# Value product of the attention by whole heads: 512-column matmuls in four parts, landing buffers for two heads

## The reference

```python
C_q = Q @ Wq_d                                  # [4, 512, 128]
C_kv = K @ Wkv_d                                # [4, 1601, 64]
CqWqk = (C_q @ W_qk).reshape(b, n, 16, 64)
scores = jnp.einsum('bnhl,bkl->bhnk', CqWqk, C_kv) / 8
attn = jax.nn.softmax(scores, axis=-1)
V_up = (C_kv @ Wv_u).reshape(b, nkv, 16, 64)
out = jnp.einsum('bhnk,bkhd->bnhd', attn, V_up)
```

## Time and profile before

| what | us |
|---|---|
| timed runs, median (lowest, highest) | 2739.88 (2732.51, 2740.12) |
| the profiled execution's own time | 2740.16 |
| its span, first to last instruction | 2738.2 |
| mixer and start of the attention | 324.55 |
| the 255 steps of the attention, first to last second-half score product | 1078.08 |
| from there to the first matmul of the feed-forward network | 27.61 |
| feed-forward network | 1307.96 |

### The profile page before, as it was taken

One profiled execution on the slowest core, in us unless ns is written; L12 is line 12 of the kernel. 1 busy time (PEld: TensorE's weight loads), 2 busy tenths in 40 slices (PEclk: granted clock), 3 DMA queues, 4 the chain that ended last, 5 costly groups with the idle time before them and its releaser, 6 DMA issues.

```text
span 2738.2 us, 42011 instructions
## 1 busy us (share of the span) xinstructions
PE 2602.3 (95%) x14328; PEld 1979.5 (72%) x14328; DVE 2315.4 (85%) x2664; ACT 1670.2 (61%) x2619; POOL 1966.1 (72%) x1473
## 2 busy tenths in 40 slices
PE   7998899999999999999988999999999999999997
PEld 4665666666666666666656888888888888788885
DVE  2766688989998999899857999899998899899988
ACT  3444687877787778787855445454455555555553
POOL 1002377677777778777857999999887888888883
PEclk9899999999999999999999999999999999999999
DMA  7426677687778776877681222112223222132221
GB/s 276 157 100 206 212 236 216 188 240 206 223 214 261 206 219 204 259 228 221 201 278 69 100 93 93 70 70 70 77 70 123 77 85 78 70 116 79 83 93 77
DMA packets 166792, 420.64 MB, mean 154 GB/s; under 512 B 30130, under 2 KB 57652, under 8 KB 166068
## 3 DMA queue, kind: packets, MB, share of 16 engines
q1 hardware_dynamic: 164276, 409.57, 47.2%
q10 hardware_dynamic: 2304, 8.39, 0.8%
HBM read 248.43 MB, written 75.04 MB: 118 GB/s over the span
## 4 chain that ended last, share of the span: by engine, by line
PE 44%; SPq 3%; DVE 2%; POOL 1%; issue 1%; ACT 1%; DMA 1%; POOLq 0%; ACTq 0%; DVEq 0%
PE c_ps L1610 42%; SPq L912 2%; PE c_ps L1622 1%; DVE c_sum_g L1766 0%; DVE c_stats L1826 0%; DMA c_ident<-in_ident 0%; POOL b_rw L1357 0%; PE c_ps L1631 0%; POOL c_sum_g L1851 0%; PE b_po L1038 0%; PE b_sc L1019 0%; DVE c_acc L1766 0%; DMA b_rz<-in_c_dz 0%; DMA b_rz<-in_c_gz 0%; ACT c_sg L1674 0%
## 5 line engine op out<-in xcount | busy, mean ns | idle before, releaser
L1766 DVE SCALAR_TENSOR_TENSOR c_acc<-c_ps,c_sd,c_acc 128x1024 f32<-128x1024 f32 x440 | 562.9, 1282 | 90.8 <-PE c_ps L1610 90.7
L1668 ACT ACTIVATE c_scaled<-c_ps,c_sgu 128x1024 f32<-128x1024 f32 x336 | 375.2, 1117 | 422.5 <-PE c_ps L1610 414.7
L1101 ACT ACTIVATE b_pr<-b_sc,b_nm 128x799 f32<-128x799 f32 (+1 forms) x512 | 477.7, 935 | 169.4 <-DVE b_pr L1190 146.9
L1851 POOL TENSOR_TENSOR c_sum_u<-c_sum_u,c_scaled 128x1024 f32<-128x1024 f32 x168 | 404.8, 2410 | 99.6 <-ACT c_scaled L1668 98.3
L1851 POOL TENSOR_TENSOR c_sum_g<-c_sum_g,c_scaled 128x1024 f32<-128x1024 f32 x168 | 405.1, 2411 | 73.2 <-ACT c_scaled L1668 72.2
L1019 PE MATMUL b_sc<-b_kh,b_qs 128*128 128x402 f32 (+1 forms) x1024 | 398.6, 389 | 45.0 <-ACT b_pr L1101 41.2
L1197 DVE STREAM_TRANSPOSE b_tn<-b_pr 128x1280 f32<-128x1280 f32 x256 | 385.4, 1506 | 28.7 <-ACT b_pr L1101 14.6
L1315 POOL COPY b_pt<-b_tn 32x640 f32<-32x640 f32 x430 | 307.4, 715 | 141.7 <-DVE b_tn L1197 82.5
L1019 PE MATMUL b_sc<-b_kl,b_qs 128*128 128x402 f32 (+1 forms) x1024 | 355.9, 348 | 0.0
L1766 DVE SCALAR_TENSOR_TENSOR c_sum_g<-c_ps,c_sgu,c_sum_g 128x1024 f32<-128x1024 f32 x224 | 286.4, 1278 | 26.0 <-PE c_ps L1610 20.6
L1190 DVE TENSOR_SCALAR_CACHE_REDUCE b_pr<-b_sc,b_nm_first 128x799 f32<-128x799 f32 x256 | 268.7, 1050 | 29.1 <-PE b_sc L1019 8.3
(11 more groups left out here) (212 smaller groups left out, 4871.0 us busy)
## 6 DMA issues: line engine op xcount, KB each, us to landing
b_pt<-b_tn SPq DMA_DIRECT2D x774, 80.0 KB, 2.7
shared<-b_tn SPq DMA_DIRECT2D x378, 80.0 KB, 2.8
c_uw_int<-wint_u SPq DMA_DIRECT2D x56, 512.0 KB, 3.5
c_gw_int<-wint_g SPq DMA_DIRECT2D x56, 512.0 KB, 3.4
c_dw_int<-wint_d SPq DMA_DIRECT2D x56, 512.0 KB, 3.4
a_cx<-in_b_ctxT SPq DMA_DIRECT2D x16, 1608.0 KB, 9.8
b_rw<-in_c_gw SPq DMA_DIRECT2D x28, 512.0 KB, 4.1
b_rz<-in_c_gz SPq DMA_DIRECT2D x28, 512.0 KB, 5.6
```

The costliest lines, as they stand in the source:

```text
L1101: S.activation(pr[u % 2][:, k0:k1], sc[:, at + lo:at + hi], ACT.Exp, bias=nm[:, u % 2:u % 2 + 1], accum_out=den[:, g % 2, q, half:half + 1 ...
L1668: S.activation(dst[:, :], pair[SLOT[x, t] % 4][:, :], ACT.Identity, scale=scale(x, t)).then_inc(s_e, 1)
L1766: V.scalar_tensor_tensor(out=total, in0=pair[SLOT[x, t] % 4][:, :], scalar=scale(x, t), in1=before, op0=ALU.mult, op1=ALU.add).then_inc(s_ ...
L1851: G.tensor_tensor(total, total, scaled[m % 2][:, :], ALU.add).then_inc(s_add, 1)
```

## The change

The value product is made per head. `weigh(g, part)` takes the four units of a head together, 512 columns in each matmul, 13 matmuls per head, in four parts over four steps: tiles 10 to 12 (those that PE turned), then 0 to 3, 4 to 6 and 7 to 9. The half of `b_po` is chosen by a running count (`z = n % 2`). The first part stands in steps 7 and 3 (`WEIGH_AT = 7`), the last in steps 2 and 6. The copy of the product out of PSUM moves one step later (`LATENT_AT = 10`, steps 2 and 6); the output product stays in steps 3 and 7.

The landing buffers hold two heads (`b_pt` and a part of `shared`): a mover may start on a pair when the head two before has been weighed, and PE waits for the two pairs of a head at once, in its second part. `b_pe` has two buffers of a head, freed after the first part by a semaphore of its own. To make room, `b_ot` and some small tiles move into `shared`, tiles of the feed-forward network are laid out in another order, its first gate weights are loaded at the end of the attention's last pair and no longer in the pairs before, and some semaphores of the mixer are merged. The weight blocks skip pairs 17, 20, 23 and 26 of a batch and no longer 20 to 23.

```diff
-FREE = (2, 5, 8, 11, 14, 20, 21, 22, 23, 30, 31)
+FREE = (2, 5, 8, 11, 14, 17, 20, 23, 26, 30, 31)
-WEIGH_AT = 6
-LATENT_AT = 9
+WEIGH_AT = 7
+WEIGH_PARTS = [(10, 11, 12), (0, 1, 2, 3), (4, 5, 6), (7, 8, 9)]
+LATENT_AT = 10
 OUT_AT = 11
-MOVES = 3
...
+        def landing(p, a, c):
+            z = p % 2 * 2
+            return pt[p // 2 % 2][32 * c:32 * c + 32, a, z:z + 2, :]
+
+        def landing_free(eng, p):
+            if p >= 4:
+                eng.wait_ge(s_pv, p // 2 - 1)
...
-            def weigh(p, part):
-                b, s, g = p // 2 // HEADS, p % 2, p // 2
+            def weigh(g, part):
+                b = g // HEADS
                 if part == 0:
-                    moved(T, p)
-                    T.wait_ge(s_pe, 2 * p + 2)
-                    if s == 0 and g:
+                    T.wait_ge(s_pe, UNITS * (g + 1))
+                    if g:
                         T.wait_ge(s_ot, g)
...
-                for t in (range(0, 7), range(7, NKT))[part]:
-                    z = t % 2
+                elif part == 1:
+                    moved(T, 2 * g)
+                    moved(T, 2 * g + 1)
+                for n, t in enumerate(WEIGH_PARTS[part], sum(len(x) for x in WEIGH_PARTS[:part])):
+                    z = n % 2
...
-                    ins = T.matmul(po[z * LAT:(z + 1) * LAT, s * 256:(s + 1) * 256], cn[:, b, t, :], turned,
-                                   start=(t < 2), stop=(t >= NKT - 2))
-                if part == 1:
+                    ins = T.matmul(po[z * LAT:(z + 1) * LAT, :], cn[:, b, t, :], turned,
+                                   start=(n < 2), stop=(n >= NKT - 2))
+                if part == 0:
+                    ins.then_inc(s_pa, 1)
+                elif part == len(WEIGH_PARTS) - 1:
                     ins.then_inc(s_pv, 1)
...
             def out_latent(g):
-                S.wait_ge(s_pv, 2 * g + 2)
+                S.wait_ge(s_pv, g + 1)
...
-FIRST = [("u", 0), ("g", 0)]
+FIRST = [("u", 0)]
...
                     Q.dma_start(sgu[:, :, :], d["gus"]).then_inc(s_scales, 16)
+                    load("g", 0)
```

More of the change, by code:

```diff
@@ L221, in sync @@
                 Q.wait_ge(s_kvout[k], 4 * 4 * 16)
-            Q.wait_ge(s_early, 32)
+            Q.wait_ge(s_wts, 64)
         def tensor():
-            T.wait_ge(first, 32)
             for l in range(L):
-                T.wait_ge(xin[l + 1 if l else 0], 16)
+                T.wait_ge(xin[l + 1 if l else 0], 16 if l else 48)
                 for c in range(KC):
@@ L409, in scalar @@
                     S.wait_ge(small, 10 * 16)
[L410 to L413, removed]
+                    S.wait_ge(s_prep, 3)
+                    S.activation(alog[:, :], alog[:, :], ACT.Exp).then_inc(s_soft, 1)
+                    S.activation(g1[:, :], g1[:, :], ACT.Sigmoid).then_inc(s_soft, 1)
+            S.wait_ge(s_prep, 6)
             def keep_context(pair):
@@ L859, in attention @@
         tn = [sb(f"b_tn{j}", [P, 4, 2, SEG]) for j in range(2)]
-        pt = [sb(f"b_pt{j}", [P, 4, 2, SEG]) for j in range(2)]
-        pt.append(shared[:, NXC + 2 * NSZ - 8 * SEG:NXC + 2 * NSZ].rearrange("p (a z e) -> p a z e", a=4, z=2))
-        pe = [sb(f"b_pe{j}", [P, NKT - NDT, 2, P]) for j in range(3)]
-        ot = sb("b_ot", [P, NB])
+        pt = [sb("b_pt0", [P, 4, UNITS, SEG])]
+        end = NXC + 2 * NSZ
+        pt.append(shared[:, end - 16 * SEG:end].rearrange("p (a u e) -> p a u e", a=4, u=UNITS))
+        ot = shared[:, end - 16 * SEG - NB:end - 16 * SEG]
+        pe = [sb(f"b_pe{j}", [P, NKT - NDT, UNITS, P]) for j in range(2)]
         yo = sb("b_yo", [P, 2, QT, LAT])
@@ L866, in attention @@
         nm0 = sb("b_nm_first", [P, 2])
-        den = sb("b_den", [P, 2, QT, 2])
-        rd = sb("b_rd", [P, 2, QT])
+        small = shared[:, end - 16 * SEG - NB - 32:end - 16 * SEG - NB]
+        den = small[:, 0:16].rearrange("p (a q z) -> p a q z", a=2, q=QT)
+        rd = small[:, 16:24].rearrange("p (a q) -> p a q", a=2)
+        var, step = small[:, 24:28], small[:, 28:32]
         stats = sb("b_stats", [P, QT, 2, 6])
@@ L1104, in keep_turned @@
             def keep_turned(u):
+                g = u // UNITS
                 S.wait_ge(s_tr, u + 1)
-                if u >= 6 and u % 2 == 0:
-                    S.wait_ge(s_pv, u // 2 - 2)
-                S.copy(pe[u // 2 % 3][:, :, u % 2, :], mi[:, 0:(NKT - NDT) * P].rearrange("p (t e) -> p t e", e=P)).then_inc(s_pe, 1)
+                if g >= 2 and u % UNITS == 0:
+                    S.wait_ge(s_pa, g - 1)
+                S.copy(pe[g % 2][:, :, u % UNITS, :], mi[:, 0:(NKT - NDT) * P].rearrange("p (t e) -> p t e", e=P)).then_inc(s_pe, 1)
             def cross(p):
@@ L1465, in ffn @@
         sgu = sb("c_sgu", [P, 2 * KC, NI])
-        part = {n: [sb(f"c_sum_{n}{j}", [P, HALF]) for j in range(2)] for n in "gu"}
-        scaled = [sb(f"c_scaled{j}", [P, HALF]) for j in range(2)]
         sg = sb("c_sg", [P, HALF])
-        h = sb("c_h", [P, HALF])
         stats = sb("c_stats", [P, OR, 2, 6])
@@ L1472, in ffn @@
         rstd = sb("c_rstd", [P, OR])
-        d1 = sb("c_dw_int1", [P, HID], F32R)
-        w = {"g": [sb("c_gw_int0", [P, HID], F32R)], "u": [sb("c_uw_int0", [P, HID], F32R)]}
-        for n in "gu":
+        h = sb("c_h", [P, HALF])
+        w = {n: [sb(f"c_{n}w_int0", [P, HID], F32R)] for n in "ug"}
+        part = {n: [sb(f"c_sum_{n}{j}", [P, HALF]) for j in range(2)] for n in "gu"}
+        scaled = [sb(f"c_scaled{j}", [P, HALF]) for j in range(2)]
+        for n in "ug":
             w[n].append(sb(f"c_{n}w_int1", [P, HID], F32R))
-        w["d"] = [sb("c_dw_int0", [P, HID], F32R), d1]
+        w["d"] = [sb(f"c_dw_int{j}", [P, HID], F32R) for j in range(2)]
         xs = sb("c_xs", [P, XR, HID])
```

85 lines of the change are left out of this document (40 added, 45 removed).

## The result

The changed kernel takes 2751.4 us (median of 13 runs, 2743.7 to 2754.8) against 2739.9 (13 runs): a ratio of 1.0040, 95% interval 1.0028 to 1.0052, so 8 to 14 us slower. The prediction was 2754. The profiled execution of after took 2746.63 us, only 6.5 us more than the profiled one of before; its span, 2744.3, is 6.1 us longer. What is missing to the 11.5 us of the medians lies ahead of the attention, whose second-half score of step 0 starts at 318.44 in place of 324.55, 6.1 us earlier. What follows compares stages and steps, not spans.

A forecast was written before the change was run, and what follows sets the result against it. The attention was where time could move, with no engine near its limit. 0.66 us per cycle over 32 cycles gave 21 us, less 7 for landing buffers: +14 on 2740.2, so 2754 us, with 2741 to 2773 for 8 in 10.

The forecast's parts named there:

- Step 7: Attention's regular eight-step cycle: PE fills this step, so 0.42 us more, plus a new 0.12 us wait of `output` for ACT's copy.
- step 3: Attention's regular cycle: PE fills this step, so 0.42 us more, less 0.09 us for a restart that goes; no new wait.
- steps 1 and 2: Attention's regular cycle: PE's wait for ACT's exponential goes, so 7.86 us becomes 7.67, a gain of 0.19.
- steps 5 and 6: Attention's regular cycle: the chain from ACT's copies of the queries keeps its length, so 8.75 us stays; change 0.
- steps 0 and 4: Attention's regular cycle: value product of four matmuls takes 1.86 us instead of 1.87, so 0.01 us less each.
- Weight blocks: Attention's weight-block copies and their pair spacing: 0, at worst 2 us in each of three batches.
- Landing buffers: Attention's irregular part, 25 us outside the regular cycle: slack for every second pair and longer pairs take back 7 us.
- the irregular time: Rival: all 25 us outside the attention's regular cycle go, giving 2736 us; chance 0.13 (most of it, 2734 to 2748).
- The lone matmul found no partner: Rival, value product: next instruction's records run beside the odd matmul, giving 2720 us; chance 0.06, shared with other waits gone.
- The cheap wide record: Rival, value product: 512 columns take only 0.215 us, DVE then holds the attention, giving 2672 us; chance 0.01.
- no odd step hides anything: Rival, attention: odd steps pass on PE's added work and `output` waits 0.35 us, cycle 2.0 us longer, 2804 us; chance 0.07.
- The hidden ending: Attention's end: last head's landed tiles take 4.3 us instead of 3.0, hidden by the 3.9 us wait before the feed-forward network.

## Why the prediction was right, and where it wasn't

The value product came out term by term. Step 7 grew by 0.60 us (0.42 and the wait of 0.12 predicted, 0.18 measured), step 3 by 0.32 (0.33 predicted), steps 1 and 2 fell by 0.21 (0.19), steps 5 and 6 stayed at 8.74, steps 0 and 4 are unchanged: 0.71 us a cycle against 0.66, 22.7 us against 21. The reason is shown three ways: taking a lone matmul away (steps 3 and 7, 0.856 us), halving it by a split in both halves (0.42), and making one half deeper (0.85). PE's busy time grew by 42 us and not by the 52 of work: for one, step 1 of before counts as busy for the whole of its 3.55 us, of which the prediction found 3.42 to be work. Of the 42 us by which PE's busy time grew, 29 filled waits for ACT that are gone (41.2 to 12.4), and the other 13 lengthen the stage.

Two small terms were wrong, and that they cancelled is luck. "Weight blocks" stood at 0, and was worth 7 to 9 us to the good. "Landing buffers" stood at -7, a gain that no run shows: with the old spacing the irregular part didn't shrink (26.8 against 25.1), though the times leave room for it. The step that failed is the reading of the earlier trace rows: it was seen that row loads push the exchange back, not that a block in the same pair, whose store has to land, makes SyncE's turn longer than the pair (9.04 us against 8.44), nor that `FREE` decides how many such pairs follow each other. For the spacing only POOL's normalised rows were weighed.

Of the rivals, the irregular time did pay some, 9 of 25 us, by another mechanism than the one argued. The lone matmul found no partner by itself. Given one by a split in the same parts it brings less than that case priced: a cycle of 32.89, where it foresaw some 32.6, and 2733 us in place of 2720; 2716.5 took the parts 3, 3, 4, 3 as well. The cheap wide record is refuted. The Trainium skill's price for a matmul alone (TensorE: Matmul & The Clock Gate, section Back-to-back issue gap), which the prediction says the records follow, fits them in proportion to the columns only: as an estimate by it 512 columns would take 0.216 us, and a record takes 0.43. That no odd step hides anything is refuted too: the cycle grew by 0.71 and not by 2.0 us, since steps 1 and 2 need 7.65 us, less than the 7.86 of before. The hidden ending held, with nothing left over: the last product took 6.00 us in place of the 4.3 worked out, at a granted clock of 0.75 after a wait of 4.43 us for the last landing.

What stays open: how much the second pair's landing slack is worth by itself, since it wasn't tried without the wide records; where the spacing acts in the kernel before; and which share of the 6 us between the two profiled starts is chance.

## What to carry to other kernels

Count a product in column halves by its deeper half per scheduled part, not by its instructions: an odd matmul costs a pair, and splitting its columns over both halves gives the time back (here 18 us and more). When a shortening of one engine doesn't reach the end, look at the DMA-issuing queue's work per pair against the pair's length. Put free places where the queue's other work is; and look whether a slower clock follows a long PE wait, since it can cost as much as the wait.

## What the runs showed of the hardware that wasn't expected

Some waits of PE cost about as much again, or more, through the clock: after 2.81 us without work (parts 3, 3, 4, 3) the step behind ran at 0.54, and after 1.9 us in the kernel with the split lone matmul too:

```profile
844.64:850.18 5.54, 3.64 (x23) 2.08 (x21) 4.75 (x5) 3.61 (x8) 4.16 (x5) 1.00 0.99 359
850.18:857.64 7.46, 7.46 (x28) 5.29 (x28) 4.15 (x8) 3.65 (x8) 4.35 (x6) 0.54 0.79 281
```

Other waits weren't followed by a fall. In the kernel with parts 2, 3, 4, 4 a wait of 2.52 us (it ends at 819.90) was followed by a step of 4.06 us at 1.00, and in the kernel before waits of 0.82 and 1.77 us in one step by a step of 4.30 us at 1.00. What sets the two kinds apart isn't shown. Such pairs of wait and slow step are part of why the irregular part rose to 34 to 41 us in four of the kernels with a shorter cycle: with parts 3, 3, 4, 3 the steps at a granted clock below 0.9 and the steps ahead of them hold 22 of the 39.4 us, in the kernel before 3 of 25.1. That the waits come more often because landings come later within a shorter cycle is a guess.
